# The shift and scale of one layer norm moved from VectorE to GpSimd and ScalarE, with new order words

## The chip, the core and the metric

The kernel runs on one core of a Trainium2 chip. The metric is the device time of one execution in microseconds. Engine names in the profile: PE is TensorE (PEld its weight loads), DVE is VectorE, ACT is ScalarE, POOL is GpSimd, SP is SyncE, which here issues every DMA.

## The reference

Sixteen sequences of 512 rows and 128 columns pass through two residual blocks, all in float32.

```python
x = x + _layernorm(_L0_attn_ref(_layernorm(x), ...))   # state space block
x = x + _layernorm(_L0_ffn_ref(_layernorm(x), ...))    # two attention + feed-forward layers

def step(state, ts):                    # the state space block, per time step
    da = jnp.exp(dt_t[:, :, None] * a)
    dbu = dt_t[:, :, None] * b_t[:, None, :] * u_t[:, :, None]
    state = da * state + dbu
    y_t = jnp.einsum('bds,bs->bd', state, c_t)
def _layer(x, ...):                     # two of these
    h = shift_token(x);  q, k, v = split(h @ wqkv)
    q, k = rotary_xpos(l2norm(q) * qs, l2norm(k) * ksc)
    x = x + local_attention(q, k, v) @ wo
    h = layernorm(shift_token(x)) * lg + lb
    a, g = split(h @ w1 + b1);  x = x + (a * gelu(g)) @ w2 + b2
```

The change concerns the inner `_layernorm(x)` of the second line, the norm ahead of the first attention: (x - mean) * rs, where rs is 1 / sqrt(variance + 1e-5).

## The kernel before

Each sequence is one 128 x 4 x 128 tile (128 partitions, four blocks of 128 rows). It goes through streams of work, each of which is a generator on every engine: E enters (first norm, input projection, convolution, gates), F forms the step sizes (`dt`, `du`), M scans the states and ends the first block, A is the first attention and feed-forward layer (tiles with `f_bank`), B is the second (tiles with `b_bank`), C is the last norm and the output. Five things run at once: M and A of one sequence, B of the sequence before it, E of the next one. S on SP stores what E made.

The order in which one engine issues the instructions of these streams is fixed before the run. `weave` walks a word such as `"B5 M1 B1 A3 ..."`: each part lets a stream advance by so many steps (a step ends at a `yield`), and the word is repeated until the streams are empty. A second word gives how many steps a stream is skipped at first. One pass of the word is one sequence, so one pass is called a period. Engines run their own lists strictly in order and wait for each other by semaphores, so an instruction that waits holds all behind it.

**The scan (M).** For each of 32 groups ACT makes `da` (L609), POOL makes `dbu` (L663), DVE scans `hs` (L629), POOL multiplies with C into `gy` (L680), PE sums (L584). The data come by DMA from the scratch `steps` into three slots of `spread`.

**The seam.** After the last scan come: DVE `gate` (L621), POOL `gate` (L687), PE `da` (L592, the output projection), DVE `stat_y`, `mv_y` (L317, L322), ACT `lv_y`, `rs_y` (L329, L333), DVE `gy` (L642, that norm applied), POOL `x` (L691, the residual added: the tile x1), DVE `stat_x`, `mv_x`, ACT `lv_x`, `rs_x`, DVE `xs` (L652, four `tensor_scalar`: the norm of the change), PE turns `xs` (L357 `f_bank<-first,xs`), ACT copies it (L819, L821), PE projects (L720), ACT squares (L832), DVE rotates (L928, L932, L942). POOL clips the sums of squares `ss` (L988) and scales `kr` (L997). In the same stretch E and F of the next sequence pass: PE L449 (input projection), L453 (B, C and step rows), L460 (steps), ACT L497, L504, L507, DVE L423, POOL L430 and L435, the stores of `steps` and the loads of `spread`. B ends there (L1028, L1031 and L1039 are its and A's expansion and contraction, L1069 gelu, L1085 gating, L1089 the residual), and C: DVE `stat_out`, `mv_out`, `mr_out` (L338), ACT `xs` (L352), POOL `xs` (L1146).

**The same norm elsewhere.** Two forms exist in the code. With the first, DVE subtracts the mean and multiplies (L642, L652). With the second, an engine forms `mr` = -mean * rs, and ACT applies it as scale and bias (`act_normalise`, L352). For the norm at the entry (`n_e`), POOL forms `mr` in two operations (L343, L346, `pool_enter`); for the others DVE does in one (L338).

Of the kernel before, what the change touches and what calls it, by code (L numbers as in the profile page):

```python
# [10 lines left out]
ALU = mybir.AluOpType  # L11
# [5 lines left out]
NT = T // P  # L17
# [30 lines left out]
    "act": (  # L48
# [5 lines left out]
    "dve": (  # L54
# [5 lines left out]
    "pool": (  # L60
        "M5 A1 M1 A2 M12 E1 M31 F4 C1 B2 M1 A1 M3 A1 B1 A1 B1 M4 A1 B2 M2 A2 B1 M3 B2 M2 A1 M3 B3 A2",
        "A27 B36 C4 E1 F4 M116"),
    "sp": (
        "M3 A1 M8 S2 B1 M1 C1 S1 F2 M9 B1 A1 B1 M1 E1",
        "A5 B10 C5 E0 F2 M34 S3"),
# [42 lines left out]
def build(nc, a, out):  # L108
    with ExitStack() as ctx:
# [163 lines left out]
        x_loaded, e_normed = sig("x_loaded", 1, 16), sig("e_normed", 1)  # L273
        e_negated, e_shifted = sig("e_negated", 1), sig("e_shifted", 1)
# [65 lines left out]

        def pool_enter(E, e, b):
            E.wait_ge(*n_e.measured(b, 1))
            e.tensor_scalar(n_e.mr[:, :], n_e.mv[:, :, 0], -1.0, None, ALU.mult).then_inc(e_negated.sem, 1)  # L343
            E.wait_ge(*n_e.scaled(b, 1))
            E.wait_ge(*e_negated(b))
            e.tensor_tensor(n_e.mr[:, :], n_e.mr[:, :], n_e.rs[:, :], ALU.mult).then_inc(e_shifted.sem, 1)  # L346
            yield

        def act_normalise(E, e, w, b, dst, src):
            E.wait_ge(*(e_shifted(b) if w is n_e else w.measured(b, 2)))  # L350
            for t in range(NT):
                op = e.activation(dst(t), src(t), ACT.Identity, bias=w.mr[:, t:t + 1], scale=w.rs[:, t:t + 1])  # L352
            return op
# [244 lines left out]
        def act_state(E, e, b):  # L598
# [14 lines left out]
            yield from act_norm_scale(E, e, n_x, b)  # L613

        def dve_state(E, e, b):
# [32 lines left out]
            E.wait_ge(*n_x.scaled(b, 1))  # L648
            if b > 2:
                E.wait_ge(*stored(b - 3))  # L650
            for t in range(NT):
                op = e.tensor_scalar(xs[b % 3][:, t, :], x1[:, t, :], n_x.mv[:, t, 0:1], n_x.rs[:, t:t + 1], ALU.subtract,  # L652
                                     ALU.mult)
            op.then_inc(x2_made.sem, 1)
            yield
# [451 lines left out]
        def pool_front(E, e, b):  # L1107
            yield from pool_attention(E, e, b, wf)
# [214 lines left out]
```

## Time and profile before

| | us |
|---|---|
| median of 3 runs (2418.8 to 2420.0) | 2419.76 |
| the profiled execution's own time | 2425.17 |
| its span, first to last instruction | 2423.4 |
| PE busy | 1934.9 (80%) |
| DVE busy | 1914.2 (79%) |
| ACT busy | 1741.6 (72%) |
| POOL busy | 1716.1 (71%) |

Busy time is an average over stretches with different limits. To read it, look at one period: the sixteen additions L691 start between 147.3 and 2192.5 us, and those shown here lie 136.94 us apart (407.06 and 544.00).

### The profile page before, as it was taken

To read this page: it belongs to the slowest core of one execution; us is meant where nothing else is said; L and a number is where in the kernel's file an instruction comes from. 1 tells how busy PE (TensorE), PEld (TensorE's weight loads), DVE (VectorE), ACT (ScalarE), POOL (GpSimd) and SP (SyncE) were. 2 spreads that over 40 slices of the span, in tenths; PEclk is the share of its full clock that TensorE was granted. 3 is DMA by queue.
4 is the path that set the end of the run, shared out by engine and by line. 5 is a ranking of instruction groups with operands and counts; after the bars stand their busy time and mean duration, and the time that the engine had idled before them with its cause. 6 is when DMAs were issued, how large, how long until landed. Compare 5 with 4: busy or idle time off the path is not lost.

```text
span 2423.4 us, 43963 instructions
## 1 busy us (share of the span) xinstructions
PE 1934.9 (80%) x15823; PEld 1138.6 (47%) x15936; DVE 1914.2 (79%) x3509; ACT 1741.6 (72%) x3891; POOL 1716.1 (71%) x1572
## 2 busy tenths in 40 slices
PE   2255889798988979797988979797988979788866
PEld 0012446363635446363645546363644536364634
DVE  3557797979889797988888797988889797987442
ACT  2245778696978778696877879696877869686644
POOL 1959596877959596886959596895959597792110
PEclk9967999998999999899999989999999999899988
DMA  5444343535345453535434353534434353541000
GB/s 167 126 114 119 107 119 96 131 101 145 100 118 131 107 123 89 142 82 151 113 110 122 108 125 95 142 91 132 124 105 119 106 133 94 140 104 34 17 16 14
DMA packets 126346, 261.09 MB, mean 108 GB/s; under 512 B 26928, under 2 KB 59696, under 8 KB 125872
## 3 DMA queue, kind: packets, MB, share of 16 engines
q1 hardware_dynamic: 126128, 258.27, 40.4%
q8 instruction: 126, 2.06, 0.4%
q14 instruction: 92, 0.75, 0.1%
HBM read 185.42 MB, written 42.99 MB: 94 GB/s over the span
## 4 chain that ended last, share of the span: by engine, by line
PE 37%; ACT 18%; DVE 18%; POOL 14%; issue 10%; DMA 2%; SPq 0%; POOLq 0%; DVEq 0%; ACTq 0%
POOL dbu L663 5%; POOL gy L680 5%; ACT late L893 4%; DVE m L928 4%; PE b_bank L357 3%; PE f_bank L357 3%; ACT da L609 3%; DVE kr L942 3%; PE b_bank L763 2%; POOL kr L997 2%; PE y_sum L584 2%; PE b_bank L780 2%; PE b_bank L746 2%; PE f_bank L746 2%; PE f_bank L763 2%
## 5 line engine op out<-in xcount | busy, mean ns | idle before, releaser
L629 DVE TENSOR_TENSOR_SCAN hs<-da,dbu 128x512 f32<-128x512 f32 x512 | 623.3, 1217 | 112.5 <-POOL dbu L663 67.6
L680 POOL TENSOR_TENSOR gy<-hs,bc 128x512 f32<-128x512 f32 x512 | 652.7, 1275 | 34.2 <-DVE hs L629 21.8
L663 POOL TENSOR_TENSOR dbu<-spread,bc 128x512 f32<-128x512 f32 x512 | 652.2, 1274 | 16.5 <-DMA spread<-steps 16.5
L609 ACT ACTIVATE da<-spread,rest 128x512 f32<-128x512 f32 x512 | 362.3, 708 | 140.2 <-DVE hs L629 121.1
L720 PE MATMUL b_bank<-rest,h_t 128*128 128x512 f32 x384 | 245.8, 743 | 75.4 <-DVE kr L942 71.5
L997 POOL TENSOR_TENSOR kr<-kr,rn 128x512 f32<-128x512 f32 x256 | 261.0, 1044 | 32.9 <-ACT rn L853 18.4
L720 PE MATMUL f_bank<-rest,h_t 128*128 128x512 f32 x384 | 235.8, 717 | 40.2 <-DVE kr L942 30.4
L584 PE MATMUL y_sum<-gy,rest 128*32 128x512 f32 x1024 | 146.4, 647 | 93.3 <-POOL gy L680 93.3
L357 PE MATMUL b_bank<-first,kr 128*128 128x128 f32 x768 | 127.5, 291 | 82.3 <-DVE kr L942 60.4
L893 ACT ACTIVATE late<-b_bank,mx 128x128 f32<-128x128 f32 x512 | 141.0, 383 | 60.5 <-DVE mx L958 60.5
L1146 POOL TENSOR_TENSOR xs<-xs,v 128x512 f32<-128x512 f32 x16 | 18.9, 1183 | 215.9 <-ACT xs L352 215.9
L357 PEld LDWEIGHTS b_bank<-first,kr 128*128 128x128 f32 x768 | 88.7, 146 | 170.4 <-DVE kr L942 105.8
L720 PEld LDWEIGHTS b_bank<-rest,h_t 128*128 128x128 f32 x384 | 77.5, 228 | 171.0 <-DVE kr L942 102.5
L357 PE MATMUL f_bank<-first,kr 128*128 128x128 f32 x768 | 129.2, 298 | 35.3 <-DVE kr L942 18.8
L720 PEld LDWEIGHTS f_bank<-rest,h_t 128*128 128x128 f32 x384 | 84.0, 234 | 153.5 <-issue 95.2
L915 DVE TENSOR_REDUCE ss<-sq 128x16 f32<-128x1024 f32 x128 | 154.6, 1208 | 0.0
L893 ACT ACTIVATE sq<-f_bank,mx 128x128 f32<-128x128 f32 x512 | 143.6, 396 | 4.9 <-DVE mx L958 4.9
L430 POOL TENSOR_TENSOR k_t<-k_t,m 128x512 f32<-128x512 f32 x32 | 40.5, 1284 | 146.3 <-ACT m L507 146.3
L357 PEld LDWEIGHTS f_bank<-first,kr 128*128 128x128 f32 x768 | 90.6, 150 | 80.5 <-DVE kr L942 52.3
L357 PE MATMUL b_bank<-first,late 128*128 128x128 f32 x512 | 87.5, 296 | 46.7 <-ACT late L893 46.7
L928 DVE TENSOR_TENSOR m<-f_bank,tab 128x512 f32<-128x512 f32 x128 | 87.0, 680 | 44.2 <-ACT sq L832 44.0
L958 DVE TENSOR_REDUCE mx<-b_bank 128x4 f32<-128x512 f32 x128 | 83.4, 684 | 34.0 <-PE b_bank L746 32.7
(171 smaller groups left out, 4789.3 us busy)
## 6 DMA issues: line engine op xcount, KB each, us to landing
spread<-steps SPq DMA_DIRECT2D x256, 512.0 KB, 4.7
vs<-v SPq DMA_DIRECT2D x96, 260.0 KB, 5.6
steps<-k_t SPq DMA_DIRECT2D x32, 512.0 KB, 3.0
bc<-bc_rows SPq DMA_DIRECT2D x32, 512.0 KB, 6.4
gate<-gates SPq DMA_DIRECT2D x32, 512.0 KB, 5.4
gates<-kr SPq DMA_DIRECT2D x16, 512.0 KB, 2.9
gates<-late SPq DMA_DIRECT2D x16, 512.0 KB, 3.9
vs<-v SPq DMA_DIRECT2D x32, 130.0 KB, 4.7
```

Of the source, the lines that this page charges most:

```text
L357: op = e.transpose(bank[:, n * P:(n + 1) * P], src(n), ident[:, :])
L584: op = e.matmul(y_sum[32 * j:32 * j + 32, :], sel[:, w, :], gy[:, 2 * j + k, :], start=w == 0 and k == 0, stop=w == 1 and k == 1, skip_gro ...
L609: e.activation(da[:, :], spread[:, slot(b, s // 2), 0, :], ACT.Exp, scale=a_neg[:, s:s + 1]).then_inc(decayed.sem, 1)
L629: e.tensor_tensor_scan(hs[:, s % 2, :], da[:, :], dbu[:, s % 2, :], 0.0, ALU.mult, ALU.add).then_inc(scanned.sem, 1)
L663: e.tensor_tensor(dbu[:, s % 2, :], spread[:, slot(b, s // 2), 1, :], bc[:, s % 2, :], ALU.mult).then_inc(fed.sem, 1)
L680: e.tensor_tensor(gy[:, s % 8, :], hs[:, s % 2, :], bc[:, 2 + s % 2, :], ALU.mult).then_inc(read_out.sem, 1)
L720: e.matmul(bank[:, :], w.h_t[:, t * P:(t + 1) * P], wqkv[:, l, part * INNER:(part + 1) * INNER], start=True, stop=True).then_inc(w.project ...
L746: op = e.matmul(X[i][WIN * j:WIN * j + WIN, p * P:(p + 1) * P].rearrange("p (a n) -> p a n", a=2), w.q_t[r:r + DH, g, q0:q0 + WIN], keys i ...
L893: op = e.activation(w.pr[:, hd % 2, p, :], X[hd % 2][:, p * P:(p + 1) * P], ACT.Exp, bias=w.mx[:, hd, p:p + 1])
L915: e.tensor_reduce(w.ss[:, 2 * g:2 * g + 2, :], w.sq[:, :, :].rearrange("p n (h d) -> p n h d", h=HEADS), AX, ALU.add).then_inc(w.summed.se ...
L928: e.tensor_tensor(halves(w.m2[:, n % 2, :]), halves(bank[:, :])[:, :, ::-1, :], table[1], ALU.mult).then_inc(w.rotated.sem, 1)
L997: e.tensor_tensor(x, x, w.rn[:, n, :].unsqueeze(2).to_broadcast([P, HEADS, DH]), ALU.mult).then_inc(w.normed.sem, 1)
```

## The change

The DVE stage L652 (four `tensor_scalar` on 128 x 128, and two waits ahead of them) goes. POOL forms `mr_x` in two operations on 128 x 4 at the head of its A stream (`pool_shift`, also used by the entry as before); ACT applies the norm at the end of its M stream. The wait for the store of three sequences before (`stored`) moves with it. All five order words are new.

```diff
+        x_negated, x_shifted = sig("x_negated", 1), sig("x_shifted", 1)
...
+        def pool_shift(E, e, w, b, negated, shifted):
+            E.wait_ge(*w.measured(b, 1))
+            e.tensor_scalar(w.mr[:, :], w.mv[:, :, 0], -1.0, None, ALU.mult).then_inc(negated.sem, 1)
+            E.wait_ge(*w.scaled(b, 1))
+            E.wait_ge(*negated(b))
+            e.tensor_tensor(w.mr[:, :], w.mr[:, :], w.rs[:, :], ALU.mult).then_inc(shifted.sem, 1)
...
         def act_normalise(E, e, w, b, dst, src):
-            E.wait_ge(*(e_shifted(b) if w is n_e else w.measured(b, 2)))
+            E.wait_ge(*(e_shifted(b) if w is n_e else x_shifted(b) if w is n_x else w.measured(b, 2)))
...
             yield from act_norm_scale(E, e, n_x, b)
+            if b > 2:
+                E.wait_ge(*stored(b - 3))
+            act_normalise(E, e, n_x, b, lambda t: xs[b % 3][:, t, :], lambda t: x1[:, t, :]).then_inc(x2_made.sem, 1)
+            yield
...
             yield from dve_norm_stats(E, e, n_x, b, lambda t: x1[:, t, :])
-            E.wait_ge(*n_x.scaled(b, 1))
-            if b > 2:
-                E.wait_ge(*stored(b - 3))
-            for t in range(NT):
-                op = e.tensor_scalar(xs[b % 3][:, t, :], x1[:, t, :], n_x.mv[:, t, 0:1], n_x.rs[:, t:t + 1], ALU.subtract,
-                                     ALU.mult)
-            op.then_inc(x2_made.sem, 1)
-            yield
...
         def pool_front(E, e, b):
+            pool_shift(E, e, n_x, b, x_negated, x_shifted)
+            yield
             yield from pool_attention(E, e, b, wf)
...
     "pool": (
-        "M5 A1 M1 A2 M12 E1 M31 F4 C1 B2 M1 A1 M3 A1 B1 A1 B1 M4 A1 B2 M2 A2 B1 M3 B2 M2 A1 M3 B3 A2",
-        "A27 B36 C4 E1 F4 M116"),
+        "M3 A1 F4 C1 B1 A1 B2 A2 M4 B1 M2 B1 M3 A1 M2 B2 M2 B1 A1 M1 A1 M1 A1 B1 M2 B1 M1 B2 M1 A1 M2 A1 M2 A1 M1 "
+        "A2 M19 E1 M21",
+        "A26 B36 C4 E0 F4 M70"),
```

The new words show best as instruction rows. Line numbers of the changed kernel are up to 9 higher. **POOL from the residual addition on, before:** `x` is the new x1, `k_t` the steps, `summed1` and `inverse1` belong to B, those with 0 to A.

```order
L691 TENSOR_TENSOR x<-gy,x 128x512 [waits residual_loaded,y_normed]
L430 TENSOR_TENSOR k_t<-k_t,m 128x512 [waits dt_clipped,dt_log] x2
L435 TENSOR_TENSOR k_t<-k_t,late 128x512 [waits u_made,dt_made] x2
L1146 TENSOR_TENSOR xs<-xs,v 128x512 [waits x1_loaded,o_normed]
L988 TENSOR_SCALAR ss<-ss 128x16 [waits summed1]
L997 TENSOR_TENSOR kr<-kr,rn 128x512 [waits inverse1]
L663 TENSOR_TENSOR dbu<-spread,bc 128x512 [waits slot_loaded1,b_loaded]
L988 TENSOR_SCALAR ss<-ss 128x16 [waits summed0]
L663 TENSOR_TENSOR dbu<-spread,bc 128x512
L680 TENSOR_TENSOR gy<-hs,bc 128x512 [waits x1_made,scanned,c_loaded]
```

The same place on POOL in the changed kernel:

```order
L692 TENSOR_TENSOR x<-gy,x 128x512 [waits residual_loaded,y_normed]
L345 TENSOR_SCALAR mr_x<-mv_x 128x4 [waits measured_x1]
L348 TENSOR_TENSOR mr_x<-mr_x,rs_x 128x4 [waits x_negated,scaled_x1]
L435 TENSOR_TENSOR k_t<-k_t,m 128x512 [waits dt_clipped,dt_log] x2
L440 TENSOR_TENSOR k_t<-k_t,late 128x512 [waits u_made,dt_made] x2
L1149 TENSOR_TENSOR xs<-xs,v 128x512 [waits x1_loaded,o_normed]
L989 TENSOR_SCALAR ss<-ss 128x16 [waits summed1]
L989 TENSOR_SCALAR ss<-ss 128x16 [waits summed0]
L998 TENSOR_TENSOR kr<-kr,rn 128x512 [waits inverse1]
L998 TENSOR_TENSOR kr<-kr,rn 128x512 [waits added1]
L998 TENSOR_TENSOR kr<-kr,rn 128x512 [waits inverse0]
L998 TENSOR_TENSOR kr<-kr,rn 128x512 [waits added0]
```

The two small operations stand between the addition and the steps, and four `kr` instead of one stand ahead of the first `dbu`.

**PE behind the output projection, before** (`b_bank` with `m` is the input projection of the next sequence, `late` its B, C and step rows, `q_t` its steps; `vs` the contraction):

```order
L592 MATMUL da<-rest,gate 128x128 x3
L1028 MATMUL b_bank<-h_t,rest 113x512 [waits gelu_made1]
L449 MATMUL b_bank<-m,first 128x512 [waits z_made]
L1028 MATMUL f_bank<-h_t,rest 114x512 [waits f_right0,f_copied0]
L453 MATMUL b_bank<-late,first 40x512 [waits z_made]
L453 MATMUL b_bank<-late,first 40x512
L1028 MATMUL f_bank<-h_t,rest 114x512
L1031 MATMUL f_bank<-h_t,rest 114x512
L1031 MATMUL b_bank<-h_t,rest 113x512 [waits f_gated1]
L460 MATMUL b_bank<-q_t,first 128x512 [waits proj_copied]
```

The same place on PE in the changed kernel:

```order
L597 MATMUL da<-rest,gate 128x128 x3
L1032 MATMUL b_bank<-h_t,rest 114x512 [waits f_gated1]
L1029 MATMUL b_bank<-h_t,rest 113x512 [waits gelu_made1]
L454 MATMUL b_bank<-m,first 128x512 [waits z_made]
L1029 MATMUL f_bank<-h_t,rest 114x512 [waits f_right0,f_copied0]
L1032 MATMUL b_bank<-h_t,rest 113x512 [waits f_gated1]
L458 MATMUL b_bank<-late,first 40x512 [waits z_made]
L458 MATMUL b_bank<-late,first 40x512
L1029 MATMUL f_bank<-h_t,rest 114x512
L1032 MATMUL f_bank<-h_t,rest 114x512
L465 MATMUL b_bank<-q_t,first 128x512 [waits proj_copied]
```

One expansion of B (L1032 on 113 rows) now stands ahead of the B, C and step rows, and another has moved from ahead of the output projection to behind it.

**ACT from `lv_x` on, before:**

```order
L329 ACTIVATE lv_x<-mv_x,columns 128x4 [waits measured_x1]
L497 ACTIVATE m<-b_bank,first 128x512 [waits dt_projected]
L333 ACTIVATE rs_x<-lv_x 128x4 [waits scaled_x1]
L504 ACTIVATE m<-m 128x512 [waits dt_size] x2
L507 ACTIVATE m<-m 128x512 [waits dt_exp] x2
L329 ACTIVATE lv_out<-mv_out,columns 128x4 [waits measured_out]
L333 ACTIVATE rs_out<-lv_out 128x4 [waits scaled_out]
L819 ACTIVATE h_t<-f_bank 64x512 [waits x_turned0]
```

The same place on ACT in the changed kernel:

```order
L331 ACTIVATE lv_x<-mv_x,columns 128x4 [waits measured_x1]
L335 ACTIVATE rs_x<-lv_x 128x4 [waits scaled_x1]
L502 ACTIVATE m<-b_bank,first 128x512 [waits dt_projected]
L509 ACTIVATE m<-m 128x512 [waits dt_size] x2
L512 ACTIVATE m<-m 128x512 [waits dt_exp] x2
L357 ACTIVATE xs<-x,mr_x,rs_x 128x128 [waits x_shifted,stored]
L357 ACTIVATE xs<-x,mr_x,rs_x 128x128 x3
L331 ACTIVATE lv_out<-mv_out,columns 128x4 [waits measured_out]
L820 ACTIVATE h_t<-f_bank 64x512 [waits x_turned0]
```

The four new activations stand behind the logarithms of the steps and ahead of `lv_out` and of the first attention's copies.

## Rows read from the trace of the kernel before

**Rows 1.** Busy time by stretch: us, then busy us of each engine.

```profile
544.00:570.00 26.00, 22.05 (x88) 11.67 (x87) 21.31 (x47) 17.36 (x34) 9.59 (x9) 0.98 0.61 167
570.00:600.00 30.00, 23.02 (x63) 9.78 (x65) 29.95 (x41) 17.66 (x38) 29.74 (x31) 0.79 0.49 121
600.00:667.00 67.00, 60.59 (x789) 42.59 (x788) 59.85 (x114) 60.63 (x154) 65.45 (x58) 1.00 0.42 106
```

**Rows 2.** POOL in order of time, its waits in brackets: start, us, instruction.

```profile
407.06 1.26 POOL L691 TENSOR_TENSOR x<-gy,x 128x512 f32<-128x512 f32 x1 [7.69 <-DVE gy L642]
...
530.73 1.26 POOL L680 TENSOR_TENSOR gy<-hs,bc 128x512 f32<-128x512 f32 x1 [1.10 <-DVE hs L629]
...
544.00 1.26 POOL L691 TENSOR_TENSOR x<-gy,x 128x512 f32<-128x512 f32 x1 [7.68 <-DVE gy L642]
552.92 2.54 POOL L430 TENSOR_TENSOR k_t<-k_t,m 128x512 f32<-128x512 f32 x2 [7.66 <-ACT m L507]
...
563.45 1.18 POOL L1146 TENSOR_TENSOR xs<-xs,v 128x512 f32<-128x512 f32 x1 [5.54 <-ACT xs L352]
567.17 0.25 POOL L988 TENSOR_SCALAR ss<-ss 128x16 f32<-128x16 f32 x1 [2.54 <-DVE ss L915]
568.09 1.04 POOL L997 TENSOR_TENSOR kr<-kr,rn 128x512 f32<-128x512 f32 x1 [0.67 <-ACT rn L853]
569.09 1.27 POOL L663 TENSOR_TENSOR dbu<-spread,bc 128x512 f32<-128x512 f32 x1
...
602.53 4.04 POOL L997 TENSOR_TENSOR kr<-kr,rn 128x512 f32<-128x512 f32 x4 [0.58 <-ACT rn L851]
```

**Rows 3.** The chain that ended last, in this seam: start, us, what.

```profile
552.34 1.98 DVE xs L652 x4
...
556.27 0.31 ACT lv_out L329
...
559.76 0.70 DVE m L928
```

**Rows 4.** DVE in order of time, in the seam and at the first peaks.

```profile
552.25 2.07 DVE L652 TENSOR_SCALAR xs<-x,mv_x,rs_x 128x128 f32<-128x128 f32 x4
...
556.84 1.10 DVE L338 SCALAR_TENSOR_TENSOR mr_out<-mv_out,rs_out 128x4 f32<-128x4 f32 x1
...
606.74 0.85 DVE L317 BATCH_NORM_STATS2 stat_enter<-sq 128x6 f32<-128x128 f32 x4
...
608.50 1.29 DVE L958 TENSOR_REDUCE mx<-b_bank 128x4 f32<-128x512 f32 x2
```

**Rows 5.** Durations by line: ns least/median/most, first and last start.

```profile
L652 DVE TENSOR_SCALAR xs<-x,mv_x,rs_x x64: 336/341/1301, 152.8 to 2198.7; 128x128 f32<-128x128 f32 x64
```

**Rows 6.** Durations of the two POOL forms that the change adds, on other tiles.

```profile
L343 POOL TENSOR_SCALAR mr_enter<-mv_enter x16: 225/226/227, 6.6 to 2007.4; 128x4 f32<-128x4 f32 x16
...
L346 POOL TENSOR_TENSOR mr_enter<-mr_enter,rs_enter x16: 201/201/203, 7.1 to 2007.8; 128x4 f32<-128x4 f32 x16
```

**Rows 7.** ACT in order of time, in the seam.

```profile
541.98 0.30 ACT L329 ACTIVATE lv_y<-mv_y,columns 128x4 f32<-128x4 f32 x1
...
552.23 1.14 ACT L507 ACTIVATE m<-m 128x512 f32<-128x512 f32 x2
...
559.13 0.60 ACT L832 ACTIVATE sq<-f_bank 128x512 f32<-128x512 f32 x1
...
561.73 1.64 ACT L352 ACTIVATE xs<-xs,mr_out,rs_out 128x128 f32<-128x128 f32 x4
```

**Rows 8.** PE in order of time, in the seam.

```profile
540.83 1.91 PE L453 MATMUL b_bank<-late,first 128*40 128x512 f32 x4
...
543.62 1.02 PE L1031 MATMUL f_bank<-h_t,rest 128*114 128x512 f32 x2
544.48 1.02 PE L1031 MATMUL b_bank<-h_t,rest 128*113 128x512 f32 x2
...
553.07 2.84 PE L1039 MATMUL f_bank<-rest,vs 114*128 114x128 f32 x24
```

More of the change, by code:

```diff
@@ L43 @@
     "pe": (
[4 rows of a table removed]
[4 rows of a table added]
     "act": (
[5 rows of a table removed]
-    "dve": (
[5 rows of a table removed]
[5 rows of a table added]
+    "dve": (
[5 rows of a table added]
     "pool": (
-        "M5 A1 M1 A2 M12 E1 M31 F4 C1 B2 M1 A1 M3 A1 B1 A1 B1 M4 A1 B2 M2 A2 B1 M3 B2 M2 A1 M3 B3 A2",
-        "A27 B36 C4 E1 F4 M116"),
+        "M3 A1 F4 C1 B1 A1 B2 A2 M4 B1 M2 B1 M3 A1 M2 B2 M2 B1 A1 M1 A1 M1 A1 B1 M2 B1 M1 B2 M1 A1 M2 A1 M2 A1 M1 "
+        "A2 M19 E1 M21",
+        "A26 B36 C4 E0 F4 M70"),
     "sp": (
-        "M3 A1 M8 S2 B1 M1 C1 S1 F2 M9 B1 A1 B1 M1 E1",
-        "A5 B10 C5 E0 F2 M34 S3"),
+        "M1 S3 M2 F2 M6 B1 A1 M1 B1 M2 C1 M1 E1 A1 M6 B1 M3",
+        "A4 B9 C4 E0 F2 M24 S3"),
 }
@@ L339, in dve_norm_shift @@
                 w.measured.sem, 1)
-        def pool_enter(E, e, b):
[L342 to L346, printed above, removed]
+        def pool_shift(E, e, w, b, negated, shifted):
[4 more added lines that the diff above has]
+            e.tensor_tensor(w.mr[:, :], w.mr[:, :], w.rs[:, :], ALU.mult).then_inc(shifted.sem, 1)
+        def pool_enter(E, e, b):
+            pool_shift(E, e, n_e, b, e_negated, e_shifted)
             yield
         def act_normalise(E, e, w, b, dst, src):
-            E.wait_ge(*(e_shifted(b) if w is n_e else w.measured(b, 2)))
+            E.wait_ge(*(e_shifted(b) if w is n_e else x_shifted(b) if w is n_x else w.measured(b, 2)))
             for t in range(NT):
```

28 rows, old and new, of the table ORDER are left out of this document.

## The prediction

> **What bounds the kernel now.** I read first the busy shares (no engine above 80% of the span), then the list of POOL in order of time to find the period, then the busy times of three stretches of one period, and last, for the seam, the chain that ended last beside the lists of the four engines.
>
> The period is the distance of two additions of the residual, 544.00 - 407.06 = 136.94 us [rows 2]; there are sixteen, and 136.94 times 16 is 2191 of the span of 2423.4. Within it the limits change. From 600 to 667 POOL is busy for 65.45 of 67 us. From 570 to 600 both DVE (29.95 of 30) and POOL (29.74) are full, while PE is at a granted clock of 0.79 and is not waited for. From 544 to 570 nobody is full: PE has 22.05 us of work in 26, DVE 21.31, ACT 17.36, POOL 9.59, and the stretch is a chain of single waits [rows 1]. So the period is a body in which POOL sets the pace (its idle time there comes in pieces of 0.58 and 1.10 us) and a seam in which POOL sits idle for 7.68, 7.66, 5.54 and 2.54 us [rows 2]. Time is won only if the seam gets shorter or POOL has less to do in the body.
>
> In the seam the chain runs x1 (POOL, 544.00), statistics, then DVE's `xs` 552.34 for 1.98 us, `lv_out` on ACT at 556.27, the copies, `sq`, and DVE's first rotation `m` at 559.76 [rows 3]. The stage that the change takes away is a link of it, as the profile draws it. From 559.76 on DVE is full. That start, 15.76 us behind x1, is the mark to follow; the second mark is POOL's first `k_t`, 8.92 us behind x1 (552.92), the third the first `dbu`, 25.09 us behind x1 (569.09) [rows 2].
>
> **The DVE stage that goes.** Four `tensor_scalar` take 2.07 us here and 1.98 us of chain [rows 3, 4]. One takes 0.34 us as a rule, but up to 1.30 [rows 5]: at 552.92 POOL begins its long additions, and one of the four is held. The same happens to `mr_out` at 556.84, an operation on 128 x 4 that takes 1.10 us beside POOL's second pair [rows 2, 4]. So about 1 of the 2 us is a hold.
>
> The Trainium skill, in "GPSIMD Engine Reference", section "Key points", says that GpSimd and VectorE share their interfaces to SBUF, with contention when a DVE instruction is in a two-port mode or has two SBUF inputs. The held rows agree with it. By that rule moving `xs` away also frees a POOL that would otherwise have been disturbed, and the hold goes over to whichever DVE operation meets POOL next; by the row alone the full 1.98 us is saved on DVE. The sum below does not depend on the choice, for the reason that follows.
>
> **What is late instead.** DVE's next two links (`xs` L1089 and the statistics of the output) could be 1.98 us earlier, `lv_out` at 556.27 - 1.98 = 554.29. But ACT stands in the way. Its logarithms end at 552.23 + 1.14 = 553.37 before [rows 7]. PE now issues one B expansion ahead of the B, C and step rows; a pair of its instructions is 0.86 us (543.62 to 544.48), and that delays L453 from 540.83 by as much at most [rows 8]. Some of it is absorbed where ACT waits before its table load; walking the order through with the durations I get 0.5 to 0.7 us, so the logarithms end at 553.9. Then the four new activations: the same form takes 1.64 us for four [rows 7], to 555.5. `lv_out` comes behind it, 0.31 [rows 3], to 555.8. The first copy `h_t` needs a turned tile, and PE turns it behind A's contraction, which ends at 553.07 + 2.84 = 555.9 [rows 8]; with the turn it is 556.4. Before, it was 556.7: ACT went `lv_out`, `rs_out`, then copied. From there on it is the same run of copies to `sq`, which was at 559.13 [rows 7], and to `m`. The gain is thus 0 to 0.3 us; I take 0.15, since `sq` also waits for projections that PE issues in between. Of 1.98 us taken off DVE, 1.83 is given back as waiting for ACT and PE. Where neither expansion nor activations delayed anything it would be 1.98 (bound above); where ACT's 1.64 went wholly into the path, while DVE's stage was covered anyway, it would be -1.64 (bound below).
>
> **POOL's two small operations.** 0.23 + 0.20 = 0.43 us [rows 6], issued behind x1 while POOL then waits 7.66 us for the logarithms [rows 2]. The second waits for `rs_x`, which ACT now issues at once behind `lv_x`, ahead of the step exponentials; behind it on POOL stand the `k_t`, which are not ready for another 2 us. Cost 0. If `rs_x` were late, it would hold those additions; bound 0.43.
>
> **The steps.** POOL's `k_t` start when the logarithms are done: 0.7 us later than 552.92, by the expansion. They come as two pairs of 2.54 us [rows 2] and so end at 558.7 in place of 558.0, and the stores and loads that bring `spread` follow. Before, the first `dbu` was at 569.09, behind `kr`; whether the data or the engine was late there the row does not tell. POOL's `xs` of the output (563.45, waits for ACT) comes 0.9 us later, behind more work on ACT. It is hidden, because POOL then waits another 2.54 us for `ss` on DVE [rows 2], which the change leaves where it was.
>
> **The order of the first products.** In the new POOL word four `kr` stand ahead of the first `dbu`, where one did. Three more at 1.04 us [rows 2] make the first `dbu` 3.1 to 3.4 us late, about 572.5, and the first scan 3.9 late. But DVE is full in that stretch [rows 1] and rotates meanwhile, and POOL would have done those three `kr` a few operations later in any case. After the same set of work (four `kr`, three `dbu`, one `gy`) I get 577.5 against 577.3 for before. Then `gy` waits for a scan that is 0.4 late. I put this edit at -0.2 to +0.4 us, value +0.1. The cover is DVE's rotations; if these run out, the whole 3.4 is idle time of DVE.
>
> **Body.** POOL's idle pieces of 0.58 (for the scale of `kr` at 602.53) and 1.10 us (before the last `gy`) [rows 2] may go or grow with the new word; the sum of the work does not change beyond 0.43. DVE's `stat_enter` at 606.74 (0.85 us) stands behind the first `mx` now; `mx` was at 608.50, two us behind it [rows 4], so nothing is won unless the scores come earlier. I take -0.25 us for the better placing, with bounds of -1.7 (both pieces gone) and +1.0 (a new piece like the 1.10).
>
> **DMA.** The word for SP moves loads of later rows and output stores out of the seam; the load of C and B comes ahead of the step stores. From 544 to 570 the queues are busy for 0.61 [rows 1], so there is room; value 0, and since neither a stalled nor a freed queue shows in POOL's waits, bounds of a fifth of the smaller idle piece, some -0.1 to +0.1.
>
> **Sum.** Per seam -0.15 + 0 + 0.1 - 0.25 = -0.3 us. It counts in about 14 periods (the first and last have no full neighbours): -4.2. The profiled execution is at 2425.17, this gives 2421.0; it lies 5.4 above the median of the runs, 2419.76, so the runs should come to about 2416. Own range with the small bounds: -0.8 to +0.3 per seam, 2408 to 2424. A difference of 0.2%, 4.8 us, is about what can be told from nothing here, so this forecast sits at the edge.
>
> **Rivals.**
> - *The link is really gone.* ACT's part lies beside DVE's statistics of the output and the full 1.98 us shortens each seam. For it: the chain names `xs`, and ACT waits 2.9 us for `lv_out` there. Against: the walk above, with 1.64 us of activations in that very wait. 1.98 x 14 = 28, time 2392 (x16: 2388). Chance 0.17.
> - *The late scans are passed on (slower).* Place: POOL and DVE at 569 to 600. The price is the first `dbu` 3.4 us late; it decides when DVE has no rotations left, and then scans come one round late behind a POOL which has no slack in the body. Together with 0.7 us on the steps, 0.4 to 1.2 us per seam remain, mean 0.8: 14 x 0.8 = +11, time 2431. For it: DVE and POOL are both full there, so nothing makes good what is idle once. Against: the equal amount of work by 577. Chance 0.25.
> - *ACT as the bound.* The four activations are in the path to the first projections in full and nothing is saved: 1.64 x 14 = +23, time 2443. Chance 0.06.
> - *Nothing moves:* period set by the body's POOL alone, time 2420. Chance 0.12.
>
> **How the numbers follow.** My forecast has 0.40. Faster: 0.17 of the first rival and 0.22 of the forecast's 0.40 (below 2415). Same: 0.18 of the forecast, 0.12 for nothing, 0.05 of the late scans' lower end: 0.35. Slower: 0.20 of late scans and 0.06 of ACT: 0.26. The range leaves out ACT's 0.06 and a part of the full gain and of the upper end of the late scans: 2393 to 2434.
>
> **What would show it.** Right: `m` begins 15.4 to 15.8 us behind x1 (15.76 before), with the idle time before it ended by ACT; POOL's first `k_t` 9.4 to 9.7 behind x1; first `dbu` 28 to 29; `mr_out` still about 1.1 us beside POOL; the period 136.4 to 136.9. The full gain would show as `m` at 13.8; the late scans as DVE idle between 570 and 580 and a period above 137.3; ACT as the bound as `m` at 17. It would be wrong in kind if the period changed by more than 1 us with the seam's marks as forecast: then the body's order did it.

## The result, and the profile after

| | before | after |
|---|---|---|
| median of 8 runs each, us | 2420.68 (2418.80 to 2429.08) | 2430.57 (2427.17 to 2432.57) |
| ratio, 95% interval | | 1.0031 [1.0017, 1.0044] |
| profiled execution: own time, span, us | 2425.17, 2423.4 | 2431.42, 2429.6 |
| DVE busy, us | 1914.2 | 1867.1 |
| ACT busy, us | 1741.6 | 1772.7 |
| POOL busy, us | 1716.1 | 1721.2 |

The change makes the kernel slower by 0.3%. The forecast was 2416, slightly faster; 2430.57 is what the rival of the late scans gave (2431). Three kernels below had one execution far above its others (2867.55 us in e2, 6520.59 in e9, 4532.48 in e12), which is in none of the medians and ratios.

GpSimd in order of time in one period of the changed kernel, from the residual addition to the second product with C, and the end of that period; start, us, instruction, its wait in brackets. It answers to [rows 2].

```profile
406.17 1.26 POOL L692 TENSOR_TENSOR x<-gy,x 128x512 f32<-128x512 f32 x1 [8.72 <-DVE gy L651]
409.55 0.22 POOL L345 TENSOR_SCALAR mr_x<-mv_x 128x4 f32<-128x4 f32 x1 [2.12 <-DVE mv_x L324]
412.63 0.20 POOL L348 TENSOR_TENSOR mr_x<-mr_x,rs_x 128x4 f32<-128x4 f32 x1 [2.86 <-ACT rs_x L335]
415.81 2.50 POOL L435 TENSOR_TENSOR k_t<-k_t,m 128x512 f32<-128x512 f32 x2 [2.98 <-ACT m L512]
...
426.27 1.18 POOL L1149 TENSOR_TENSOR xs<-xs,v 128x512 f32<-128x512 f32 x1 [5.50 <-ACT xs L357]
429.13 0.25 POOL L989 TENSOR_SCALAR ss<-ss 128x16 f32<-128x16 f32 x1 [1.69 <-DVE ss L916]
430.25 0.24 POOL L989 TENSOR_SCALAR ss<-ss 128x16 f32<-128x16 f32 x1 [0.87 <-DVE ss L916]
430.46 4.05 POOL L998 TENSOR_TENSOR kr<-kr,rn 128x512 f32<-128x512 f32 x4
434.46 2.51 POOL L664 TENSOR_TENSOR dbu<-spread,bc 128x512 f32<-128x512 f32 x2
437.73 1.27 POOL L681 TENSOR_TENSOR gy<-hs,bc 128x512 f32<-128x512 f32 x1 [0.76 <-issue]
...
446.86 1.27 POOL L681 TENSOR_TENSOR gy<-hs,bc 128x512 f32<-128x512 f32 x1 [0.51 <-DVE hs L638]
...
530.21 1.27 POOL L681 TENSOR_TENSOR gy<-hs,bc 128x512 f32<-128x512 f32 x1 [0.95 <-DVE hs L638]
...
543.49 1.26 POOL L692 TENSOR_TENSOR x<-gy,x 128x512 f32<-128x512 f32 x1 [8.72 <-DVE gy L651]
```

VectorE at the marks of the same period; it answers to [rows 4].

```profile
420.48 0.30 DVE L340 SCALAR_TENSOR_TENSOR mr_out<-mv_out,rs_out 128x4 f32<-128x4 f32 x1 [1.69 <-ACT rs_out L335]
421.72 0.69 DVE L929 TENSOR_TENSOR m<-f_bank,tab 128x512 f32<-128x512 f32 x1 [0.93 <-ACT sq L833]
...
436.38 1.22 DVE L638 TENSOR_TENSOR_SCAN hs<-da,dbu 128x512 f32<-128x512 f32 x1
437.51 1.19 DVE L916 TENSOR_REDUCE ss<-sq 128x16 f32<-128x1024 f32 x1
438.62 1.22 DVE L638 TENSOR_TENSOR_SCAN hs<-da,dbu 128x512 f32<-128x512 f32 x1
```

ScalarE there; it answers to [rows 7].

```profile
414.08 1.14 ACT L509 ACTIVATE m<-m 128x512 f32<-128x512 f32 x2
415.12 1.14 ACT L512 ACTIVATE m<-m 128x512 f32<-128x512 f32 x2
416.16 1.64 ACT L357 ACTIVATE xs<-x,mr_x,rs_x 128x128 f32<-128x128 f32 x4
...
418.54 0.59 ACT L820 ACTIVATE h_t<-f_bank 64x512 f32<-64x512 f32 x1 [0.45 <-PE f_bank L362]
```

The marks of the prediction, in us behind x1: the first rotation `m` at 15.55 (421.72 - 406.17; before 15.76, forecast 15.4 to 15.8), the first `k_t` at 9.64 (before 8.92), the first `dbu` at 28.29 (before 25.09), and this period 137.32 (before 136.94). The first scan is at 30.2 (before 26.5), and GpSimd waits 0.76 us ahead of its first `gy`. The profile names nobody for that wait ("issue"), but the scan that it needs ends at 437.60, 0.13 us ahead of it.

**Where the time went.** The twelve periods from the third to the fifteenth addition take 1650.01 us before and 1662.14 after. They come in two lengths. Before, nine are of 136.93 to 137.10 and three of 139.04 to 139.19; after, five are of 137.27 to 137.51 and seven of 138.82 to 139.57. So 12 x 0.38 = 4.6 us come from the ordinary length, and 7 x 2.02 - 3 x 2.20 = 7.5 from more long periods: 12.1 together. The rest of the span gives 5.9 back: 0.9 up to the third addition, 2.7 in the last period, 2.3 behind it. That leaves the 6.2 between the two spans. The medians lie 9.9 apart, since the profiled execution of the kernel before is 4.5 above its median; each count of long periods here and below is of one execution.

**What a long period is.** The stretch from 60 to 75 us behind x1, first in an ordinary period of the changed kernel, then in a long one; columns as in [rows 1].

```profile
466.17:481.17 15.00, 11.55 (x146) 8.06 (x146) 13.07 (x23) 12.56 (x33) 15.00 (x15) 1.00 0.54 132
743.06:758.06 15.00, 11.49 (x134) 7.35 (x134) 11.47 (x17) 10.76 (x27) 13.72 (x14) 0.89 0.53 128
```

In the second the granted clock of TensorE is 0.89: it was at half its level for 3.4 us of the stretch (1.2 instead of 2.4 GHz). Every engine does less in the same 15 us, and GpSimd is idle for 1.28 us where it was full. Each period has two to four such spells, of 3.4 us or two or three times that, between 22 and 56 us behind x1; ordinary periods have them too. All seven long periods have one that begins between 60 and 71 us, and none of the five ordinary ones has. In three of the seven it begins at 69 us, and GpSimd's idle time comes behind 75. All three long periods of before have one at 67 or 68 us, behind a double one at 47.

### The profile page after: what moved, and what is told of

Same layout as the page of the kernel before. It is cut to its first block, busy times and chain, and to the rows that moved or that the text cites. A ratio compares the mean times of both kernels' runs of the same rounds, so it can differ in the third digit from the quotient of the medians.

```text
span 2429.6 us, 44124 instructions
## 1 busy us (share of the span) xinstructions
PE 1938.2 (80%) x15936; PEld 1129.4 (46%) x15936; DVE 1867.1 (77%) x3445; ACT 1772.7 (73%) x3955; POOL 1721.2 (71%) x1604
## 4 chain that ended last, share of the span: by engine, by line
PE 42%; ACT 17%; DVE 14%; POOL 11%; issue 9%; DMA 0%; SPq 0%; POOLq 0%; DVEq 0%; ACTq 0%
POOL dbu L664 5%; ACT late L894 4%; PE f_bank L362 4%; DVE m L929 4%; PE b_bank L362 4%; POOL gy L681 3%; PE b_bank L747 3%; POOL kr L998 3%; PE f_bank L764 3%; PE b_bank L781 3%; PE y_sum L589 3%; PE b_bank L764 2%; DVE kr L943 2%; ACT da L614 2%; DVE ss L916 2%
## 5 line engine op out<-in xcount | busy, mean ns | idle before, releaser
L721 PE MATMUL f_bank<-rest,h_t 128*128 128x512 f32 x384 | 222.9, 680 | 31.3 <-DVE kr L943 20.3
L362 PE MATMUL f_bank<-first,kr 128*128 128x128 f32 x768 | 121.5, 290 | 40.6 <-DVE kr L943 34.2
L721 PEld LDWEIGHTS f_bank<-rest,h_t 128*128 128x128 f32 x384 | 75.4, 219 | 122.6 <-issue 70.5
L959 DVE TENSOR_REDUCE mx<-f_bank 128x4 f32<-128x512 f32 x128 | 85.2, 678 | 36.7 <-PE f_bank L747 36.7
L692 POOL TENSOR_TENSOR x<-gy,x 128x512 f32<-128x512 f32 x16 | 20.2, 1262 | 130.0 <-DVE gy L651 130.0
```

Of the source, the lines that this page charges most:

```text
L362: op = e.transpose(bank[:, n * P:(n + 1) * P], src(n), ident[:, :])
L721: e.matmul(bank[:, :], w.h_t[:, t * P:(t + 1) * P], wqkv[:, l, part * INNER:(part + 1) * INNER], start=True, stop=True).then_inc(w.project ...
```

## The experiments

Fifteen kernels ran, five rounds each; their ratios are to the kernel before, with 95% intervals. "Of 13 periods" in the expectations takes in the shorter last one; the text counts the twelve ahead of it. To see where a period loses, I add up GpSimd's idle time from x1 on (time less the union of its records), for one period of each kind; x1 of the rows is at 544.00, 1652.18, 1928.95, 1501.63, 1104.32, 1804.00 and 1105.21.

| idle GpSimd since x1, us, at | 9 | 24.5 | 45 | 60 | 124 | period |
|---|---|---|---|---|---|---|
| before, ordinary | 7.66 | 16.41 | 16.57 | 17.25 | 18.88 | 136.94 |
| after, ordinary | 7.32 | 16.02 | 17.44 | 17.65 | 18.98 | 137.32 |
| after, long | 7.32 | 16.02 | 17.97 | 18.10 | 20.04 | 139.36 |
| e1, ordinary | 7.24 | 15.70 | 15.86 | 16.53 | 18.18 | 136.67 |
| e2 | 7.74 | 16.82 | 18.81 | 18.93 | 20.98 | 139.94 |
| e13, without a late spell | 7.23 | 16.40 | 16.97 | 17.60 | 18.78 | 137.74 |
| e13, long | 7.24 | 16.42 | 17.92 | 18.33 | 20.99 | 139.95 |

In these rows the long period of the changed kernel is behind the ordinary one by 0.53 us already at 45 us, ahead of the late spell.

**e1: the new norm in the old order.** The words of before, with one step more where the norm stands:

```diff
 # changed kernel's code; ORDER as before, but for
-"... E1 M1 F1 C2 ..."      act, "M63"       +"... E1 M1 F1 M1 C2 ..."   "M65"
-"... M31 F4 C1 ..."        pool, "A27"      +"... M31 A1 F4 C1 ..."     "A29"
-the M step of L652         dve, "M72"       +                           "M70"
```

> The order of the kernel before on all five engines, with only the norm changed: four activations on ACT behind the logarithms, two small operations on POOL behind x1, no DVE stage; every other row of every engine stands as before. Theory A (the cost of the change is in the new order words: the first product 3.2 us later behind x1, and more periods with a low-clock spell at 60 to 76 us behind x1, which are 2.1 us longer than the others): the norm alone is worth little, ratio to before 0.998 to 1.001, the ordinary period 136.6 to 137.0 us, long periods as seldom as before (3 of 13). Theory B (the 1.64 us on ACT and the wait for GpSimd cost what the change costs, the words hide some of it): ratio 1.003 to 1.010, ordinary period at least 137.3. Theory C (the DVE stage was a real link, the words spoil it): ratio 0.988 to 0.993, period 135.

Measured: 2410.35, ratio 0.9957 [0.9940, 0.9974]. It is faster than both kernels, by 11 and 20 us. Eleven of twelve periods are ordinary, 136.66 to 136.91, nearly all of them 136.67; `m` at 15.46; mr_x in GpSimd's wait:

```profile
1501.63 1.27 POOL L683 TENSOR_TENSOR x<-gy,x 128x512 f32<-128x512 f32 x1 [7.69 <-DVE gy L642]
1506.97 0.22 POOL L336 TENSOR_SCALAR mr_x<-mv_x 128x4 f32<-128x4 f32 x1 [4.07 <-DVE mv_x L315]
1509.01 0.20 POOL L339 TENSOR_TENSOR mr_x<-mr_x,rs_x 128x4 f32<-128x4 f32 x1 [1.81 <-ACT rs_x L326]
1510.56 2.51 POOL L426 TENSOR_TENSOR k_t<-k_t,m 128x512 f32<-128x512 f32 x2 [1.35 <-ACT m L503]
...
1526.42 1.27 POOL L655 TENSOR_TENSOR dbu<-spread,bc 128x512 f32<-128x512 f32 x1
...
1529.19 1.28 POOL L672 TENSOR_TENSOR gy<-hs,bc 128x512 f32<-128x512 f32 x1
...
1638.30 1.26 POOL L683 TENSOR_TENSOR x<-gy,x 128x512 f32<-128x512 f32 x1 [7.69 <-DVE gy L642]
```

The 0.27 us of the ordinary period are the 0.71 by which idle time falls up to 24.5 us, less the 0.43 of new work. The larger part of the gain is outside it. The two profiled executions lie 18.4 us apart. Of these, 12 x 0.27 = 3.2 are the ordinary period, 4.2 one long period where before has three, 2.5 the last period (132.95 instead of 135.45, which has a late spell), 1.3 lie ahead of the third addition and 7.1 behind the last, where TensorE is at half clock for 39 us instead of 59. Why the spells are fewer is open. e11, e12 and e14, which are e1 with one edit each, come to 2409 to 2411 too. No theory's ratio was met: 0.9957 lies between A's 0.998 and C's 0.993. The period and the few long ones are as A has them.

**e2: the old norm in the new order.** Before's code; in the new words ACT's and GpSimd's step of the norm taken out, VectorE's put ahead of `xs` L1089.

> The new order on all five engines, with the norm as before (DVE stage behind the second step product, no activations, no small operations on POOL). Theory A: as slow as the changed kernel or slower, ratio 1.002 to 1.006, ordinary period about 137.3, 5 to 8 of 13 periods long. Theory B: ratio 0.998 to 1.001. Theory C: much slower than before, 1.010 or more, since the stage comes back in an order that is bad by itself.

Measured: 2449.87, ratio 1.0117 [1.0097, 1.0136], far above what Theory A gave, and what C asked (1.010 or more). But C's condition, a real link of 2 us, is not met: in e1 the period is only 0.27 shorter. All twelve periods are long (139.8 to 140.1), each with a low-clock spell from 69 us on. So the two parts do not add: the new order costs 28 us with the old norm and 20 (2430.6 - 2410.4) with the new one; the norm gains 11 in the old order and 19 in the new.

**e3: GpSimd's word as before. e4: PE's word as before.** The rest as in the changed kernel.

> The changed kernel with GpSimd's order as before (its two small operations behind x1 kept), so that one kr and not four stands ahead of the first dbu; the other four words new. Theory A1 (the late first product is what lengthens the ordinary period): first dbu again 25 us behind x1, ordinary period 136.9 or less instead of 137.3, some 5 us less than the changed kernel, and the share of long periods as in it (7 of 13) if that hangs on PE, 3 of 13 if it hangs on POOL: then 2420 or less. Theory A2 (POOL's order does not matter since DVE is full there): within 0.1% of the changed kernel. Theory D (the words fit only together): slower than the changed kernel by 0.3% or more.

> The changed kernel with PE's order as before, so that the B, C and step rows stand again ahead of the B expansion; the other four words new. Theory A with PE as the cause of the spells: long periods fall from 7 to about 3 of 13, some 8 us less than the changed kernel, and POOL's first k_t is back at 8.9 us behind x1 from 9.6. If the spells hang on GpSimd's or VectorE's order: as many long periods as in the changed kernel, and the time within 0.1% of it. Theory D (the words fit only together): slower by 0.3% or more.

Measured: 2499.13, ratio 1.0319 [1.0295, 1.0343], and 2560.44, ratio 1.0573 [1.0550, 1.0595]. Theory D for both. In e3 every period is long, 142.9 to 143.6. The first `dbu` is back at 24.9 us, but it has nobody to serve: GpSimd waits for the scan that VectorE's new word has late.

```profile
1583.86 1.27 POOL L655 TENSOR_TENSOR dbu<-spread,bc 128x512 f32<-128x512 f32 x1
...
1592.33 1.26 POOL L672 TENSOR_TENSOR gy<-hs,bc 128x512 f32<-128x512 f32 x1 [5.77 <-issue]
```

**e5: VectorE's and GpSimd's words as before. e6: ACT's too. e7: SP's alone.**

> The changed kernel with VectorE's and GpSimd's order as before, together; PE, ACT and SP new. With GpSimd's order alone put back the first gy waited 5.8 us, because VectorE's new order has the first scan late. If the loss of the new order lies in the pair (first scan at 30.4 us behind x1 in place of 26.2): the ordinary period falls back to 136.7 to 137.0, the late low-clock spells become rare, the time is 2408 to 2414. If the loss lies in PE's and ACT's new order: period 137.3 or more and long periods as often as in the changed kernel, 2425 to 2435. If only whole sets of words fit: above 2450, with a new wait at the first products.

> The changed kernel with the order of ACT, VectorE and GpSimd as before; only PE's and SP's order is new. If PE's order is what brings spells to 60 to 76 us behind x1: as many long periods as in the changed kernel, 2420 or more, and the first k_t 0.6 us later than before. If the orders of PE and ACT must fit each other: a new wait of PE or ACT in the seam, 2440 or more. If PE's order costs nothing: 2408 to 2414.

> The changed kernel with the order of the DMA queue as before. Theory: the queue's order is not what costs; within 0.15% of the changed kernel (2427 to 2434), first dbu still 28.3 us behind x1, last wait for x1 unchanged. Rival: the new order of loads and stores delays the first slots of the scan or crowds the queues; then some 0.3 to 0.5% less than the changed kernel.

Measured: e5 2652.07, ratio 1.0945 [1.0923, 1.0966]; e6 2653.75, 1.0952 [1.0931, 1.0972], with 4.6 to 7.0 us of GpSimd's waiting for a scan near 80 us behind x1 in every period of both. Whole sets of words fit, and these mixed ones do not, so swapping the words of whole engines tells nothing about a single feature. e7: 2430.42, 1.0030 [1.0019, 1.0042], the same as the changed kernel. SP's new order does nothing measurable.

**e8: the first scan seven places earlier in the new order.**

```diff
-pool "... C1 B1 A1 B2 A2 M4 B1 ..."      +"... C1 B1 A1 B1 M2 B1 A2 M2 B1 ..."
 dve: first M step of a sequence seven places earlier; act: two
```

> The changed kernel with one edit: the first scan of a sequence is issued seven places earlier on VectorE, its da two places earlier on ACT, its first two dbu three kr earlier on GpSimd; all else as in the changed kernel. Expected if the late first scan is what lengthens the ordinary period: first dbu near 25.3 us behind x1, GpSimd's wait ahead of the first gy (0.5 to 1.3 us, which ends with the scan) gone, ordinary period 136.5 to 136.9 instead of 137.3, and 5 to 12 us off the changed kernel by the period alone. Rival: the wait moves to the second gy or to PE's first scores, and nothing is won; then 2428 to 2433. Second rival: the spells of low clock are what costs, and they stay: then only the ordinary period falls, and the number of long periods (7 of 13) stays.

Measured: 2440.63, ratio 1.0070 [1.0053, 1.0087], 10 us slower than the changed kernel. First `dbu` at 25.3, the wait ahead of the first `gy` gone, and two others come in its place:

```profile
1132.14 1.27 POOL L672 TENSOR_TENSOR gy<-hs,bc 128x512 f32<-128x512 f32 x1
...
1135.78 1.28 POOL L672 TENSOR_TENSOR gy<-hs,bc 128x512 f32<-128x512 f32 x1 [0.88 <-DVE hs L629]
...
1142.72 1.28 POOL L672 TENSOR_TENSOR gy<-hs,bc 128x512 f32<-128x512 f32 x1 [0.97 <-DVE hs L629]
```

Ordinary periods are 137.8, three of the twelve; nine are long. It is not the first scan alone that is late: the following ones stand as late in VectorE's row, which has at most 0.14 us of idle time from 33 to 45 us behind x1.

**e9: e1 with each v projection issued twice. e10: the changed kernel with a quarter of each.** e10 leaves out the values of six of eight heads. The question was what brings a spell to 60 us.

> The kernel with the old order and the new norm (2410), in which PE issues each v projection twice, with the same result: 8 more matmuls of 0.43 us a period (3.4 us of PE), four of each layer among those at 25 to 60 us behind x1, where PE waits for VectorE's kr. Theory of the clock (more PE work there puts a low-clock spell at 60 to 76 us behind x1, and such a period is 2.1 us longer): long periods rise from 1 of 13 to most, about 138.8, and the time by 15 to 27 us. Rival (the spell is only a companion, PE is not waited for there): ordinary periods stay 136.7 to 137.1 and long ones as rare as before, time 2410 to 2416. A cost in every period without a late spell would be the plain length of the added matmuls, 0.9 us where they stand in the seam's chain.

> The changed kernel, which leaves out three quarters of each v projection on PE (the values of six of eight heads are not computed): 8 times some 0.3 us less of PE a period. Theory of the clock: with less PE work at 25 to 60 us the late spells go from 7 of 13 to 0 to 3, and the time from 2430 to 2414 to 2420, while ordinary periods stay at 137.3 since they are set by VectorE's late scans. Rival (the extra long periods come from the order itself): long periods stay at 5 to 8 of 13, time above 2425.

Measured: e9 2429.4, ratio 1.0034 [1.0023, 1.0045]; e10 2438.71, 1.0072 [1.0051, 1.0092], slower than the kernel with the whole work. e9 by itself fits the theory that more work of PE brings late spells: five of twelve periods have one, where e1 has one. e10 does not: with less work six of twelve have one (seven in the changed kernel), and the clock was down for longer ahead of them. From 39 to 57 us behind x1, first the changed kernel, then e10:

```profile
861.40:879.40 18.00, 13.18 (x47) 5.78 (x46) 17.56 (x24) 10.58 (x24) 17.15 (x18) 0.81 0.59 131
```

```profile
997.67:1015.67 18.00, 13.01 (x36) 7.41 (x35) 17.45 (x24) 9.31 (x20) 17.16 (x18) 0.53 0.58 135
```

What PE did ahead of and in that low clock in e10: short turns, and waits for VectorE's `kr`.

```profile
992.74 0.66 PE L362 MATMUL b_bank<-first,kr 128*128 128x128 f32 x4 [2.87 <-DVE kr L944]
...
997.37 0.66 PE L362 MATMUL f_bank<-first,kr 128*128 128x128 f32 x4 [2.25 <-DVE kr L944]
999.68 2.50 PE L722 MATMUL b_bank<-rest,h_t 128*128 128x128 f32 x4 [1.65 <-DVE kr L944]
1003.71 1.11 PE L362 MATMUL b_bank<-first,kr 128*128 128x128 f32 x4 [1.53 <-DVE kr L944]
```

In e9 the spell at 24 us is gone, where PE now has work, but five of twelve periods have one at 67 or 68 us. Those are 138.4 to 138.7, the others 137.4 to 138.2, against e1's 136.67. So half of e9's 19 us stands in every period, spell or not (12 x 0.8). Where e10 loses its 8 us against the changed kernel is not seen: the profiled execution is the fastest of its six (2432.23), and its twelve periods take 1658.29 us, less than the 1662.14 of the changed kernel, though TensorE is at half clock for 280 us of them instead of 171.

**e11: one activation for the four, in e1** (`xs` over 512 columns with the first block's scale and shift).

> The kernel with the old order and the new norm, in which one activation over 512 columns with the first block's scale and shift stands for the four (three blocks are scaled with the wrong rows): 0.7 instead of 1.64 us on ACT. Theory: ACT's norm is not the last thing in the seam, PE's contraction of the first layer is (it ends 11.9 us behind x1, the turn of xs is behind it), so VectorE's first m stays at 15.4 to 15.5 us behind x1 and the period at 136.6 to 136.7, time 2407 to 2412. Rival: the four activations are in the path; then m comes 0.6 to 0.9 us earlier, period 136.0, time 2400.

Measured: 2409.03, ratio 0.9948 [0.9931, 0.9965]; ordinary period 136.67. Three of the four blocks are scaled with the wrong rows here. The activation ends 0.85 us earlier behind x1, and nothing follows from it:

```profile
1514.47 0.80 ACT L348 ACTIVATE xs<-x,mr_x,rs_x 128x512 f32<-128x512 f32 x1
...
1517.59 0.59 ACT L813 ACTIVATE h_t<-f_bank 64x512 f32<-64x512 f32 x1 [0.54 <-PE f_bank L355]
```

x1 was at 1505.20, so `h_t` is at 12.39, as in e1. PE's turn is the last thing, behind its contraction.

**e12: the shift by one VectorE operation, in e1.**

```diff
-            pool_shift(E, e, n_x, b, x_negated, x_shifted)      # GpSimd, at the head of A
+            dve_norm_shift(E, e, n_x, b)                        # VectorE, where L652 stood
```

> The kernel with the old order and the norm on ACT, but the shift mr_x made by one small VectorE operation (0.16 to 0.3 us, where the four tensor_scalar stood) and not by two on GpSimd (0.43 us). Theory that GpSimd's work counts fully: ordinary period 136.67 - 0.43 = 136.2 to 136.4, time 2402 to 2406. Rival: the two operations lie in a wait of GpSimd (7.2 us for the logarithms), so nothing changes: period 136.6 to 136.7, time 2408 to 2412. Second rival: VectorE's small operation waits for rs_x and holds up xs and the statistics of the output: m later than 15.5 us behind x1, period 136.9, 2414.

Measured: 2411.08, ratio 0.9961 [0.9947, 0.9974], as e1. Ordinary period 136.67; GpSimd idles for 7.66 us ahead of its first `k_t` again, and its two operations had cost nothing.

**e13: late first scans, put alone into e1. e14: B's expansion first, put alone into e1. e15: the reverse of e14 in the changed kernel.**

```diff
-pool "... C1 B2 M1 A1 M3 A1 B1 A1 ..."   +"... C1 B1 A1 B2 A2 M4 ..."               e13
-dve  "M1 B2 A1 B1 A1 M1 B1"              +"B2 A1 B1 A1 M1 B1 M1"; act: first da later
-pe   "E1 A2 B1" at L458                  +"B1 E1 A2"                              e14
```

> The kernel with the old order and the new norm, into which one feature of the new order is put: GpSimd takes both ss and four kr ahead of the first dbu, VectorE the first scan five places later, ACT its da six places later. This is the step that the prediction priced at -0.2 to +0.4 us (value +0.1). If the step was mis-sized and is the loss of the new order: first dbu at 28 us behind x1, GpSimd waiting 0.5 to 2 us for the first gy, ordinary period 137.2 to 138 in place of 136.67, time 2418 to 2432. If the step was sized rightly: period 136.5 to 137.0, time 2408 to 2414, and the loss sits elsewhere in the new words.

> The kernel with the old order and the new norm, in which PE issues B's expansion ahead of the B, C and step rows, as in the new order; one matmul moved three places. The prediction made this 0.5 to 0.7 us on the way to the logarithms. If it counts in full: first k_t 9.6 us behind x1 in place of 8.9, m 0.3 to 0.7 us later than 15.46, period 136.9 to 137.4, time 2413 to 2420. If PE's contraction covers it: m stays within 0.1 of 15.46, period 136.7, time 2408 to 2413.

> The changed kernel with the reverse: the B, C and step rows ahead of B's expansion on PE, all else new. If the moved expansion is part of the loss: first k_t 0.6 to 0.9 us earlier than 9.6, ordinary period 136.8 to 137.1 instead of 137.3, time 2420 to 2427. If ACT's new order, which takes B's gelu between the others, now waits for that expansion: gelus and contractions late, m later than 15.55, time 2431 or more. If neither: 2428 to 2433.

Measured: e13 2443.53, ratio 1.0087 [1.0065, 1.0108], 33 us above e1; e14 2410.01, 0.9960 [0.9946, 0.9973]; e15 2427.24, 1.0028 [1.0016, 1.0041]. In e13:

```profile
1129.80 0.24 POOL L980 TENSOR_SCALAR ss<-ss 128x16 f32<-128x16 f32 x1 [1.47 <-DVE ss L907]
1130.00 2.05 POOL L989 TENSOR_TENSOR kr<-kr,rn 128x512 f32<-128x512 f32 x2
1133.22 2.05 POOL L989 TENSOR_TENSOR kr<-kr,rn 128x512 f32<-128x512 f32 x2 [1.17 <-ACT rn L845]
1135.22 2.48 POOL L655 TENSOR_TENSOR dbu<-spread,bc 128x512 f32<-128x512 f32 x2
```

The second `ss` and the last two `kr` are not ready when GpSimd comes to them, and it waits with the products behind them. By 33 us behind x1 it has idled 2.2 us more than in e1 (17.92 against 15.76) in this period, and 1.2 more in the one without a late spell or a double one. That one is 137.74, 1.07 above e1's 136.67, as its idle time at 45 us is by 1.11; ten of twelve have a spell that begins between 68 and 69 us and are 139.3 to 140.3. e14 changes nothing, its first `k_t` stays 8.93 behind x1, and in e15 it stays at 9.6: the later `k_t` of the changed kernel is not the expansion's.

## Why the prediction was wrong

- **The norm** (sum -0.15 us per seam, of 1.98 taken off VectorE): right in kind and close in size. `m` came 0.21 us earlier with the change and 0.30 in e1, where the bound was 0.3; e1's period is 0.27 shorter. That PE gives back the rest is shown by e11 and by the 0.54 us that ACT waits for PE's turn. ACT's own time was put into the reckoning and was not needed in the old order: PE's contraction alone sets it. The rival with the whole 1.98 us fell, and so did the one with ACT as the bound.
- **GpSimd's two operations**, 0: right (e12).
- **The steps**, +0.7 us behind x1: the number was right (9.64 against 8.92), the cause wrong. e14 and e15 show that the expansion has no part in it. In the changed kernel PE's second step projection stands behind a part of B's contraction and starts 6.16 us behind x1 instead of 5.24; that this is the cause is read from the order, and was not tried alone.
- **The order of the first products**, "-0.2 to +0.4 us, value +0.1": **this is the step that failed.** From 24.5 to 45 us behind x1 GpSimd idles for 1.0 to 1.7 us in the five ordinary periods, where before it idles for 0.2 (0.4 in one of nine). So the term measures +0.9 to +1.6 in place of +0.1. In the period shown it is 0.76 us ahead of the first `gy` and 0.51 ahead of a later one, both for scans. The prediction counted GpSimd's work, held it to be only reordered, and let `gy` wait for a scan 0.4 us late. It had the first scan 3.9 us later (3.7 measured, 30.2 against 26.5) and took VectorE's rotations for a cover. It did not follow the scans behind the first in VectorE's row, which is nearly full, nor ask whether the four `kr` would be ready: each needs a sum from VectorE, a logarithm and an exponential from ACT. e13 puts the feature alone into e1 and costs 1.07 us in a period without a late spell, and 33 us in all. Its waits are others, though: there GpSimd waits for the second `ss` and two of the `kr`, while in the changed kernel the four `kr` run from 430.46 on without a gap and the scans are what is late. That the order is not free is shown; that the late scans alone make the loss of the changed kernel is read from its rows, and e8, which moves the first of them, did not win it back.
- **The body**, -0.25: right in kind, too small. From 45 to 124 us GpSimd idles for 1.3 to 1.9 us instead of 2.3, so the term measures -0.4 to -1.0. In the rows of the table the parts are: up to 24.5 us 0.39 less idle time, which the 0.43 of new work uses up; 1.26 more to 45 us; 0.77 less to 124. That makes some 0.5, near the 0.38 by which the ordinary period grew.
- **TensorE's clock** had no term. The prediction read 0.79 between 570 and 600 as a clock that nobody waits for, which is so there, and did not ask where the spells go when the order moves. 7.5 of the 12.1 us of the twelve periods come with spells at 60 to 71 us. Rows show that a period with one is 2 us longer and that GpSimd's idle time rises in it. No run separates the spell from what is late ahead of it, and what puts one there is open: e13 brings ten of them by the order alone, and e10 shows that less work of PE does not keep them away.
- **The queue**, 0: right (e7).

e1, a kernel with the norm and none of the new order, came within 0.03 us of the forecast's -0.3 per period (136.67 from 136.94). That is chance: of the forecast only the norm's -0.15 applies to it. The rival that won had the right place, but its total (2431, chance 0.25) was met by luck: it had 0.4 to 1.2 us in each seam, where the ordinary period grew by 0.38, and nothing for the long periods, which make more than half of the loss. Its condition was wrong too: VectorE hardly ran out of rotations (between 24.5 and 45 us behind x1 it idles for 0 to 0.6 us in ordinary periods, before for 0 to 0.3); it had the scans too far back in a nearly full row.

## What to carry to other kernels

Judge a moved operation by when its inputs are ready, on every engine that makes them, and by what is queued behind it; equal work in a stretch does not show that a reordering is free. If a change brings a new order with it, price and try the operation alone in the old order: here it gave -0.43% where both together gave +0.31%. Order lists of several engines fit each other as a set, and putting back one of them says what breaks, not what the list costs. Before a gain or loss is put down to an edit, see in which periods it lies: of e1's gain the ordinary periods have 3 us, and the rest goes with fewer low-clock spells.

## What the runs showed of the hardware

- A spell of TensorE at half clock is 3.4 us long here, or a multiple of it. It is there in the shortest periods too when it comes at 22 to 53 us behind x1, where VectorE and GpSimd are full with other work. At 60 to 71, in the phase of scores and softmax, it goes with 2 us more (0.2 to 1.3 in e9).
- Taking three quarters of a projection away from PE went with a clock of 0.53 instead of 0.81 over 18 us (one period of each). Over the twelve periods TensorE was at half clock for 280 us instead of 171, and they were 4 us shorter together; yet the median of the kernel was 8 us longer (2438.7 against 2430.6).
- A VectorE operation can be held until the GpSimd operation beside it ends. `mr_out` takes 0.16 us when GpSimd is idle. Before, it starts 0.18 us into one of the `k_t` of GpSimd and takes 1.10; in the changed kernel it starts 0.98 us into one and takes 0.30. In all thirteen cases of each it ends 0.02 us behind the `k_t`. In e1 it starts 0.1 us ahead of a `k_t`'s end and takes 0.16. The prediction expected 1.1 again; it did not ask where in the `k_t` it would start. Not every operation is held: each `stat_out` beside the same `k_t` takes 0.28 or 0.29 us in all three kernels. The `k_t` beside `mr_out`, before, changed and in e1, and `mr_out` in e1:

```profile
556.65 1.26 POOL L435 TENSOR_TENSOR k_t<-k_t,late 128x512 f32<-128x512 f32 x1
...
419.49 1.28 POOL L440 TENSOR_TENSOR k_t<-k_t,late 128x512 f32<-128x512 f32 x1
...
1514.25 1.27 POOL L431 TENSOR_TENSOR k_t<-k_t,late 128x512 f32<-128x512 f32 x1
...
1514.19 0.16 DVE L331 SCALAR_TENSOR_TENSOR mr_out<-mv_out,rs_out 128x4 f32<-128x4 f32 x1
```

Before, `mr_out` starts at 556.84 [rows 4], in the changed kernel at 420.48.
